# A cross-attention and feed-forward kernel: scores leave PSUM through a two-tensor product with a running maximum

## The chip, the cores and the metric

The kernel runs on one core of a Trainium2 chip. The metric is the device time of one execution in microseconds (us). Engines are named as in the profile: PE is the matrix engine, DVE the vector engine, ACT the scalar engine, POOL the GpSimd engine, and SP the engine that issues the DMAs.

## The reference

There are 1600 tokens of width 512, a context of 5776 rows of width 512, and 16 heads of width 32. What is computed, cut to what matters:

```
q = layernorm(x) @ Wq + bq            # 1600 x 512, per head 32
k, v = split(ctx @ Wkv + bkv)         # 5776 x 512 each
q = round_to_127_steps(q / sqrt(32))  # one step (scale) for each token and head
k = round_to_127_steps(k)             # one step for each key and head
v = round_to_127_steps(v)             # one step for each channel
attn = softmax(q @ k.T)               # per head 1600 x 5776
attn = round_to_255_steps(attn)       # scale: max(attn) / 255 of each row
x = x + (attn @ v) @ Wp + bp
x = x + ffn(layernorm(x))             # 512 -> 2 x 1408 -> 512, quantised, with an RMS norm
```

Because the rounded softmax row has its largest entry at 255, the kernel computes exp(s - max(s) + ln 255) and lets the write to an 8-bit integer do the rounding. The row sum of the exponentials divides the result later.

## The kernel before

**Stages.** First (to about 290 us) q is made for all tokens and k and v for the first group of four heads. Then comes the attention loop (about 290 to 1,780 us), and after it the output projection and the feed-forward part.

**The attention loop.** It has NA = 200 steps. A step `i` is one tile of 128 queries of one head (`tile_of`); for two heads at a time there are 25 steps, the last of which holds the two remainders of 64 queries. In a step the 5776 keys are taken in NC_ = 4 chunks of 1536, 1536, 1536 and 1168. For each chunk:

1. PE (`scores`, line 593) multiplies the queries `QT` with the keys `KT` into one of two PSUM buffers `PS`, up to three matmuls of 512 columns. It may write a buffer when the chunk two before has been evicted (semaphore `s_ev`).
2. DVE (line 967) evicts the chunk: it reads `PS`, multiplies by the query's step with its sign turned (`SQN`, or `SQP` in the tile of remainders), writes the negated scores as f32 to `S` in SBUF, and keeps their minimum in `MN`. The instruction is followed by a read of the accumulator.

After the four chunks DVE (line 982) forms `MS` = min of (`MN` + ln 255), which is the offset ln 255 - max(score), and signals `s_mx`. ACT (line 791) then computes exp(-S + MS) over the whole tile of 5888 columns to 8-bit integers `Pr`. The columns behind key 5776 hold `PAD_SCORE`, so that their exponential is 0. SP (line 464) transposes `Pr` by DMA to `PP`, POOL (line 1155) unpacks it to `PT` in four casts, and PE (`values`, line 612) multiplies it with the values `VI`, four steps (LAG) behind the scores. ACT (line 777) takes the product out of PSUM to `AO`, and PE waits for that (`s_pve`) before it writes `PO` again.

`S`, `MN`, `MS`, `Pr`, `PP` and `PT` have two buffers each. DVE may write `S[i % 2]` when the exponential of step i - 2 is done (`s_exp`).

**Beside it** the loop makes k and v of the next group of four heads, in 12 batches for each of three groups: PE lines 540 to 547, ACT lines 712 and 714 (out of PSUM), DVE lines 878 to 885 between two evictions, POOL lines 1091 to 1112, ACT lines 720 to 737. At a group's end POOL also quantises v (lines 1124 and 1127).

**Order.** Every engine has one queue, written out by hand in the order of the loops; an instruction that waits holds up all behind it on its engine. In ACT's queue a step is: the exponential, what is due of k (lines 737, 720 and 725), k and v out of PSUM for the next step, and the output of the tile i - 3 (line 777). In PE's queue each chunk's `scores` stand ahead of a quarter of `values(i - 4)`, and a part of the work for k and v stands behind.

Of the kernel before, what the change touches and what calls it, by code (L numbers as in the profile page):

```python
# [39 lines left out]
P = 128  # L40
# [24 lines left out]
PAD_SCORE = 1.0e30  # L65
# [48 lines left out]
class Chain:  # L114
# [13 lines left out]
    def link(self, ins):  # L128
        self.mark(ins)
        self.sync()  # L130


def build(nc, x, ctxt, ctxl, Wq, bq, Wkv, bkv, Wp, bp, w13T, w2T, norm_w, eye, Qd, Kd, Vd, Od, out):
    ctx = ExitStack()
    with ctx:
# [20 lines left out]
        MJ = sb("MJ", [P, NC_], F32)  # L156
        st = sb("st", [P, 2, 8], F32)
# [55 lines left out]
        with ExitStack() as unsplit:  # L213
# [27 lines left out]
                   s_kr s_kn s_ki s_kc s_k6 s_k8 s_kh s_kd s_kl s_kp s_vd0 s_vd1 s_vr s_vt s_vg s_vi s_wp s_qk s_ev s_mx s_exp s_pad s_pvp s_pv s_pve s_rz  # L241
# [456 lines left out]
        def _(act):  # L698
# [87 lines left out]
            for i in range(NA + LAG - 1):  # L786
                if i < NA:
                    act.wait_ge(M["s_mx"], i + 1)
                    if i >= 2:
                        act.wait_ge(s_tr[i % 2], 16 * (i // 2))  # L790
                    act.activation(Pr[i % 2].rearrange("p t q b -> p t b q"),  # L791
                                   S[i % 2].rearrange("p (t b q) -> p t b q", b=2, q=P), ACT.Exp, bias=MS[:, i % 2, 0:1],
                                   scale=-1.0, accum_out=ZB[:, i:i + 1]).then_inc(M["s_exp"], 1)
                for g, b in dve_batches.get(i - K_SPLIT, []):
                    k_high(g, b)
                for g, b in dve_batches.get(i - K_CAST, []):
                    k_round(g, b)
                for u in UNITS.get(i + 1, []):
                    unit_out(*u)
                if i >= LAG - 1:  # L800
                    values_out(i - LAG + 1)
# [49 lines left out]
        def _(v):  # L851
# [12 lines left out]
            link(v.memset(VF[:, (NU - 1) * P:KP], 0.0))  # L864
            v.memset(KS, 0.0).then_inc(M["cst"], 1)
# [51 lines left out]
            for t in range(NT):  # L917
# [13 lines left out]
                v.tensor_scalar(SQN[:, t, :], am[:, 1, :], -1.0 / 127.0, None, ALU.mult)  # L931
# [25 lines left out]
            for i in range(NA):  # L957
                p, segs = tile_of(i)
                h, q0 = segs[0][0], segs[0][1]
                neg_step = SQN[:, q0 // P, h:h + 1] if len(segs) == 1 else SQP[:, p:p + 1]  # L960
                if i >= 2:
                    v.wait_ge(M["s_exp"], i - 1)
                for c in range(NC_):
# [3 lines left out]
                    v.tensor_scalar(S[i % 2][:, c * CHUNK:c * CHUNK + CW[c]], PS[n % 2][:, 0:CW[c]], neg_step, None,  # L967
                                    ALU.mult, ALU.min, accum_out=MN[:, i % 2, c:c + 1]).then_inc(M["s_ev"], 1)
# [13 lines left out]
                v.tensor_scalar(MJ[:, :], MN[:, i % 2, :], LN255, None, ALU.add, ALU.min,  # L982
# [274 lines left out]
```

## Time and profile before

| what | before |
|---|---|
| median time (2 runs) | 2090.84 us (2090.33 to 2091.34) |
| profiled execution, its own time | 2093.51 us |
| its span | 2091.7 us |
| busy: PE, DVE, ACT, POOL | 1750.2, 1674.7, 1355.6, 1497.3 us |
| evictions, line 967 (with accumulator reads) | 1285.8 us |
| exponentials, line 791 | 1041.5 us |
| unpacking casts, line 1155 | 1096.2 us |
| score matmuls, line 593 | 789.5 us |
| TensorE's mean granted clock | 0.836 of full speed |

The profiled execution is 2.67 us longer than the median. Busy times are sums over records, and two DVE records can overlap by some tens of ns, so that DVE's real occupation is somewhat less than its busy share.

### The profile page before, as it was taken

The numbers are of one execution on the slowest core, as the hardware profiler recorded it, in microseconds if no ns is written. First come the engines' busy times: TensorE is split into PE (matmuls) and PEld (weight loads), VectorE is DVE, ScalarE is ACT, GpSimd is POOL, SyncE is SP. The second block draws the span as 40 slices with busy tenths as digits, with TensorE's granted clock in tenths as the row PEclk, the third lists the DMA queues.
The fourth block names the chain that finished last, engine by engine and source line by source line (L and its number), as shares of the span: only waits on it lengthen the run. The fifth ranks groups of instructions, "written<-read, shape, count | busy, mean of one in ns | idle before, by whom it ended". The sixth has DMA issues, their size and how long they took to land.

```text
span 2091.7 us, 40535 instructions
## 1 busy us (share of the span) xinstructions
PE 1750.2 (84%) x16230; PEld 1183.8 (57%) x16230; DVE 1674.7 (80%) x2664; ACT 1355.6 (65%) x1293; POOL 1497.3 (72%) x1182
## 2 busy tenths in 40 slices
PE   7765678898887888888788888978989889589997
PEld 6654456666565666655566665434444444367774
DVE  5433679999997999998799999989999999355552
ACT  2212268888868888887688888777777777332221
POOL 1211339888989888888898889988897987344543
PEclk9887789999898999988899999555555655699998
DMA  5333469999998989999988999897976875613221
GB/s 169 101 121 102 142 145 195 201 181 201 190 221 172 198 178 190 174 181 214 194 172 178 212 180 178 185 170 129 184 137 116 159 130 104 197 45 74 53 63 41
DMA packets 862442, 323.11 MB, mean 154 GB/s; under 512 B 789104, under 2 KB 817712, under 8 KB 862256
## 3 DMA queue, kind: packets, MB, share of 16 engines
q1 hardware_dynamic: 862256, 320.53, 73.5%
q8 instruction: 129, 2.11, 0.4%
q14 instruction: 57, 0.47, 0.1%
HBM read 80.87 MB, written 46.20 MB: 61 GB/s over the span
## 4 chain that ended last, share of the span: by engine, by line
DVE 34%; PE 26%; POOL 13%; issue 12%; DMA 7%; ACT 5%; SPq 3%; POOLq 0%; DVEq 0%; ACTq 0%
DVE S L967 30%; POOL PT L1155 8%; PE PS L593 6%; PE PS L654 5%; DMA PP<-Pr 3%; PE PK L540 3%; PE PK L688 3%; DMA k_rows<-KS 2%; PE PS L570 2%; PE PK L671 2%; ACT Pr L791 2%; PE PK L542 2%; PE PO L612 1%; POOL VQ L1124 1%; SPq L464 1%
## 5 line engine op out<-in xcount | busy, mean ns | idle before, releaser
L967 DVE TENSOR_SCALAR_CACHE_REDUCE S<-PS,SQN 128x1536 f32<-128x1536 f32 (+1 forms) x768 | 1285.8, 1714 | 93.4 <-PE PS L593 78.0
L791 ACT ACTIVATE Pr<-S,MS 128x5888 uint8<-128x5888 f32 x200 | 1041.5, 5207 | 245.0 <-DVE MJ L982 171.8
L1155 POOL CAST PT<-PP 128x1536 uint16<-128x1536 uint8 (+1 forms) x800 | 1096.2, 1416 | 94.5 <-DMA PP<-Pr 93.5
L593 PE MATMUL PS<-KT,QT 96*128 96x512 bf16 (+1 forms) x2496 | 789.5, 448 | 115.3 <-DVE S L967 101.7
L612 PEld LDWEIGHTS PO<-VI,PT 128*128 128x128 f16 x9200 | 365.3, 102 | 360.7 <-issue 188.4
L612 PE MATMUL PO<-VI,PT 128*128 128x32 bf16 x9200 | 376.7, 183 | 95.1 <-ACT AO L777 67.7
L593 PEld LDWEIGHTS PS<-KT,QT 96*128 96x128 bf16 (+1 forms) x2496 | 216.1, 108 | 314.6 <-issue 183.5
L540 PE MATMUL PK<-WG,CT 128*128 128x128 f32 (+1 forms) x1272 | 233.6, 316 | 85.3 <-ACT VF L714 56.4
L540 PEld LDWEIGHTS PK<-WG,CT 128*128 128x128 f32 (+1 forms) x1272 | 183.4, 210 | 90.8 <-issue 70.0
L542 PE MATMUL PK<-CT,WG 128*128 128x128 f32 (+1 forms) x1272 | 215.3, 298 | 0.0
L542 PEld LDWEIGHTS PK<-CT,WG 128*128 128x128 f32 x1272 | 171.5, 199 | 1.3 <-issue 0.5
L654 PE MATMUL PS<-W,XIF 128*128 128x512 f32 (+3 forms) x624 | 142.6, 384 | 4.1 <-POOL XIF L1210 4.1
L1112 POOL TENSOR_TENSOR KS<-KE 128x512 bf16<-128x512 f32 (+1 forms) x48 | 50.0, 1041 | 128.5 <-DMA k_rows<-KS 124.4
L654 PEld LDWEIGHTS PS<-W,XIF 128*128 128x128 f32 (+1 forms) x624 | 113.2, 186 | 31.2 <-POOL XIF L1210 6.1
L1091 POOL TENSOR_TENSOR KB<-KB,kam 128x512 f32<-128x512 f32 (+1 forms) x48 | 48.6, 1013 | 106.9 <-DVE kam L885 106.9
L737 ACT ACTIVATE KS<-KD 128x512 bf16<-128x512 bf16 (+1 forms) x48 | 29.2, 609 | 116.7 <-DMA k_rows<-KS 113.5
L712 ACT ACTIVATE KB<-PK 128x128 f32<-128x128 f32 (+1 forms) x159 | 42.7, 269 | 90.8 <-PE PK L542 89.9
L1103 POOL TENSOR_TENSOR KD<-KE,kam 128x512 f32<-128x512 f32 (+1 forms) x48 | 50.8, 1058 | 67.0 <-ACT KE L725 67.0
L906 DVE RECIPROCAL sd<-sd 128x1 f32<-128x1 f32 x13 | 2.1, 164 | 114.3 <-ACT sd L743 114.3
L688 PE MATMUL PK<-W,IQF 128*128 128x512 f32 (+1 forms) x286 | 71.9, 409 | 15.1 <-POOL IQF L1204 11.5
L688 PEld LDWEIGHTS PK<-W,IQF 128*128 128x128 f32 (+1 forms) x286 | 54.8, 193 | 29.5 <-POOL IQF L1204 12.4
L843 ACT ACTIVATE TG<-G 128x1408 f32<-128x1408 f32 (+1 forms) x13 | 17.9, 1377 | 79.9 <-DVE G L1044 79.9
(125 smaller groups left out, 1484.5 us busy)
## 6 DMA issues: line engine op xcount, KB each, us to landing
CT<-ctxt SPq DMA_DIRECT2D x180, 256.0 KB, 3.3
k_rows<-KS SPq DMA_DIRECT2D x44, 512.0 KB, 3.9
v_rows<-VS SPq DMA_DIRECT2D x33, 256.0 KB, 3.7
VQ<-v_rows SPq DMA_DIRECT2D x33, 256.0 KB, 3.7
q_rows<-QS SPq DMA_DIRECT2D x13, 512.0 KB, 3.0
W13F<-w13T SPq DMA_DIRECT2D x16, 352.0 KB, 4.2
attn_out<-AO SPq DMA_DIRECT2D x8, 416.0 KB, 4.5
PP<-Pr SPq DMA_TRANSPOSE x200, 5.9
```

The lines of the kernel that those rows point to most:

```text
L540: pe.matmul(bank[0:n, 0:GC], CT[k % RING][:, d, 0:n], WG[:, d, 0, :], start=(d == 0), stop=False)
L542: last = pe.matmul(bank[:, GC:GC + n], WG[:, d, 1, :], CT[k % RING][:, d, 0:n], start=(d == 0), stop=(d == NK - 1))
L593: last = pe.matmul(PS[n % 2][p0:p0 + r, f:f + w], QT[h % 3][0:PARTS * HD, q0:q0 + r], KT[h % 3][0:PARTS * HD, c * CHUNK + f:c * CHUNK + f ...
L612: last = pe.matmul(PO[:, 0:w], PT[i % 2][:, u, :].bitcast(F16), VI[g % 2][:, u, h * HD:h * HD + w], start=(u == 0), stop=(u == NU - 1))
L654: last = pe.matmul(PS[half][0:n, f:f + w], XIF[:, c, 0:n], W13[:, c, a, half * FF + f:half * FF + f + w], start=(c == 0 and a == 0), stop= ...
L688: last = pe.matmul(PK[0:n, :], IQF[:, k, 0:n], W2[:, k, a, :], start=(k == 0 and a == 0), stop=(k == NF - 1 and a == WPARTS - 1))
L791: act.activation(Pr[i % 2].rearrange("p t q b -> p t b q"), S[i % 2].rearrange("p (t b q) -> p t b q", b=2, q=P), ACT.Exp, bias=MS[:, i % ...
L967: v.tensor_scalar(S[i % 2][:, c * CHUNK:c * CHUNK + CW[c]], PS[n % 2][:, 0:CW[c]], neg_step, None, ALU.mult, ALU.min, accum_out=MN[:, i % ...
L1091: gp.tensor_tensor(KA, KA, kam[:, kb % 2, 1, 0:m].unsqueeze(2).to_broadcast([P, m, HD]), ALU.mult).then_inc(M["s_kn"], 1)
L1103: gp.tensor_tensor(v3(KD), v3(KE), kam[:, kb % 2, 0, 0:m].unsqueeze(2).to_broadcast([P, m, HD]), ALU.mult).then_inc(M["s_k6"], 1)
L1112: gp.tensor_tensor(KS[:, 0:n, :, 2 * HD:3 * HD].rearrange("p n h d -> p (n h) d"), v3(KE), top(KE), ALU.subtract).then_inc(M["s_kp"], 1)
L1155: gp.tensor_copy(PT[i % 2][:, 2 * t0:2 * t1, :].rearrange("p (t b) q -> p t b q", b=2), PP[i % 2][:, t0:t1, :].bitcast(U8).rearrange("p t ...
```

## The change

Five edits:

- The eviction of a chunk is another instruction, now at line 975: `S = (PS * ONE) * step`, with `ONE` a block of ones in SBUF as a second tensor, and a running maximum that starts at -1e30, written to `MN`. It has an accumulator read behind it.
- The sign of the step is positive, `S` holds the scores themselves, and `PAD_SCORE` is -1e30.
- The last reduction (line 991) is a maximum over the four entries of `MN`, multiplied by 1.0; ln 255 is no longer added in it.
- ACT makes the offset: a new instruction (line 792) computes `BS` = -`MS` + ln 255 on 128x1, signals `s_bs`, and the exponential waits for that, with scale 1 and offset `BS`. It stands behind the wait for `s_mx` and ahead of the wait for the transposition.
- At the start DVE fills `L255` (128x1) and `ONE` (128x1536) in the row of memsets that all engines wait for (`cst`).

```diff
-PAD_SCORE = 1.0e30
+PAD_SCORE = -1.0e30
@@ tensors
+        BS = sb("BS", [P, 2, 1], F32)
+        L255 = sb("L255", [P, 1], F32)
+        ONE = sb("ONE", [P, CHUNK], F32)
@@ scalar engine, attention loop
                     act.wait_ge(M["s_mx"], i + 1)
+                    act.activation(BS[:, i % 2, :], MS[:, i % 2, :], ACT.Identity, bias=L255[:, 0:1],
+                                   scale=-1.0).then_inc(M["s_bs"], 1)
                     if i >= 2:
                         act.wait_ge(s_tr[i % 2], 16 * (i // 2))
+                    act.wait_ge(M["s_bs"], i + 1)
                     act.activation(Pr[i % 2].rearrange("p t q b -> p t b q"),
-                                   S[i % 2].rearrange("p (t b q) -> p t b q", b=2, q=P), ACT.Exp, bias=MS[:, i % 2, 0:1],
-                                   scale=-1.0, accum_out=ZB[:, i:i + 1]).then_inc(M["s_exp"], 1)
+                                   S[i % 2].rearrange("p (t b q) -> p t b q", b=2, q=P), ACT.Exp, bias=BS[:, i % 2, 0:1],
+                                   scale=1.0, accum_out=ZB[:, i:i + 1]).then_inc(M["s_exp"], 1)
@@ vector engine, start
             link(v.memset(VF[:, (NU - 1) * P:KP], 0.0))
+            link(v.memset(L255[:, :], LN255))
+            link(v.memset(ONE[:, :], 1.0))
             v.memset(KS, 0.0).then_inc(M["cst"], 1)
@@ vector engine, quantisation of q
-                v.tensor_scalar(SQN[:, t, :], am[:, 1, :], -1.0 / 127.0, None, ALU.mult)
+                v.tensor_scalar(SQN[:, t, :], am[:, 1, :], 1.0 / 127.0, None, ALU.mult)
@@ vector engine, attention loop
-                neg_step = SQN[:, q0 // P, h:h + 1] if len(segs) == 1 else SQP[:, p:p + 1]
+                step_ = SQN[:, q0 // P, h:h + 1] if len(segs) == 1 else SQP[:, p:p + 1]
...
-                    v.tensor_scalar(S[i % 2][:, c * CHUNK:c * CHUNK + CW[c]], PS[n % 2][:, 0:CW[c]], neg_step, None,
-                                    ALU.mult, ALU.min, accum_out=MN[:, i % 2, c:c + 1]).then_inc(M["s_ev"], 1)
+                    v.tensor_tensor_reduce(S[i % 2][:, c * CHUNK:c * CHUNK + CW[c]], PS[n % 2][:, 0:CW[c]],
+                                           ONE[:, 0:CW[c]], step_, -1.0e30, ALU.mult, ALU.max,
+                                           accum_out=MN[:, i % 2, c:c + 1]).then_inc(M["s_ev"], 1)
...
-                v.tensor_scalar(MJ[:, :], MN[:, i % 2, :], LN255, None, ALU.add, ALU.min,
+                v.tensor_scalar(MJ[:, :], MN[:, i % 2, :], 1.0, None, ALU.mult, ALU.max,
                                 accum_out=MS[:, i % 2, 0:1]).then_inc(M["s_mx"], 1)
```

No instruction changes its place. On DVE the end of a step and the start of the next read so before (the accumulator reads, which the trace shows, are not listed here):

```order
L967 TENSOR_SCALAR S,MN<-PS,SQN 128x1536 x3
L967 TENSOR_SCALAR S,MN<-PS,SQN 128x1168
L982 TENSOR_SCALAR MJ,MS<-MN 128x4
L967 TENSOR_SCALAR S,MN<-PS,SQN 128x1536
L878 TENSOR_REDUCE kam<-KB 128x16
```

and so in the change, from a step's third chunk on:

```order
L975 ISA S,MN<-PS,ONE,SQN 128x1536
L975 ISA MN 128x1
L975 ISA S,MN<-PS,ONE,SQN 128x1168
L975 ISA MN 128x1
L991 TENSOR_SCALAR MJ,MS<-MN 128x4
L975 ISA S,MN<-PS,ONE,SQN 128x1536
L975 ISA MN 128x1
L886 TENSOR_REDUCE kam<-KB 128x16
```

The new eviction is a pair, the product and the read of the accumulator into `MN`. On ACT, at the start of the attention loop, the change reads:

```order
L792 ACTIVATE BS<-MS,L 128x1
L797 ACT_TABLE_LOAD
L797 ACTIVATE Pr,ZB<-S,BS 128x23x2x128
L715 ACTIVATE KB<-PK 128x4x32
L717 ACTIVATE VS<-PK,BV 128x128
L792 ACTIVATE BS<-MS,L 128x1
```

The small instruction `BS` is new in front of each exponential, and no further table load comes with it.

## Rows read from the trace of the kernel before

**Rows 1.** The page: the chain that ended last, by engine and by line.
```profile
DVE 34%; PE 26%; POOL 13%; issue 12%; DMA 7%; ACT 5%; SPq 3%; POOLq 0%; DVEq 0%; ACTq 0%
DVE S L967 30%; POOL PT L1155 8%; PE PS L593 6%; PE PS L654 5%; DMA PP<-Pr 3%; PE PK L540 3%; PE PK L688 3%; DMA k_rows<-KS 2%; PE PS L570 2%; PE PK L671 2%; ACT Pr L791 2%; PE PK L542 2%; PE PO L612 1%; POOL VQ L1124 1%; SPq L464 1%
```

**Rows 2.** Windows: stretch, length, busy time of each engine, granted clock, DMA share, GB/s.
```profile
590.00:660.00 70.00, 54.91 (x602) 38.50 (x601) 55.63 (x85) 47.29 (x44) 63.41 (x61) 0.88 1.01 200
...
1500.00:1779.00 279.00, 248.82 (x2344) 124.75 (x2342) 268.98 (x397) 212.34 (x122) 238.13 (x169) 0.55 0.71 132
sum 1489.00, PE 1291.55 PEld 828.84 DVE 1396.59 ACT 1202.54 POOL 1300.70; mean PE 143.51 PEld 92.09 DVE 155.18 ACT 133.62 POOL 144.52
```

**Rows 3.** Timeline of DVE in the loop: start, duration (us), line, operation.
```profile
303.54 1.82 DVE L967 TENSOR_SCALAR_CACHE_REDUCE S<-PS,SQN 128x1536 f32<-128x1536 f32 x1
305.28 0.08 DVE L967 DVE_READ_ACCUMULATOR S<-PS,SQN 128x1 f32 x1
...
310.33 1.82 DVE L967 TENSOR_SCALAR_CACHE_REDUCE S<-PS,SQN 128x1536 f32<-128x1536 f32 x1
...
312.08 0.70 DVE L878 TENSOR_REDUCE kam<-KB 128x16 f32<-128x528 f32 x1
312.69 1.81 DVE L967 TENSOR_SCALAR_CACHE_REDUCE S<-PS,SQN 128x1536 f32<-128x1536 f32 x1
```

**Rows 4.** DVE by line and form: count | busy us, mean ns of one | idle before.
```profile
L967 DVE TENSOR_SCALAR_CACHE_REDUCE S<-PS,SQN 128x1536 f32<-128x1536 f32 x576 | 1025.8, 1814 | 93.1 <-PE PS L593 77.9 <-ACT Pr L791 14.2 <-issue 0.6
L967 DVE TENSOR_SCALAR_CACHE_REDUCE S<-PS,SQN 128x1168 f32<-128x1168 f32 x192 | 271.6, 1414 | 0.3 <-PE PS L593 0.2
...
L1044 DVE SCALAR_TENSOR_TENSOR G<-PS,sc,TG 128x1408 f32<-128x1408 f32 x12 | 20.2, 1683 | 51.0 <-PE PS L654 51.0
...
L926 DVE TENSOR_TENSOR QF<-PS,BQ 128x512 f32<-128x512 f32 x13 | 9.0, 692 | 7.9 <-PE PS L570 7.5
...
L909 DVE TENSOR_SCALAR XN<-XT,mv,sd 128x512 f32<-128x512 f32 x13 | 7.1, 546 | 0.5
...
L1022 DVE TENSOR_SCALAR Y<-Y,sc 128x512 f32<-128x512 f32 x12 | 5.8, 487 | 0.4
```

**Rows 5.** Chain of waits, its pieces in order of time: start, us, what.
```profile
783.38 0.10 DVE MJ L982
...
783.52 5.08 issue
...
790.40 0.10 ACT AO L777
...
792.10 1.28 PE PS L593 x3
```

**Rows 6.** Timeline of DVE: the eviction that this chain reaches, idle before it.
```profile
793.42 1.82 DVE L967 TENSOR_SCALAR_CACHE_REDUCE S<-PS,SQN 128x1536 f32<-128x1536 f32 x1 [1.40 <-PE PS L593]
```

**Rows 7.** Chain of waits: the first and last exponential that follow line 982 on it.
```profile
399.98 5.08 issue
...
1771.39 5.30 ACT Pr L791 x2
```

**Rows 8.** ACT, line 743: durations in ns, least/median/most, first and last start.
```profile
L743 ACT ACTIVATE sd<-mv x13: 186/187/204, 17.3 to 220.7; 128x1 f32<-128x1 f32 x13
```

**Rows 9.** Waits over the span: us in total, times, longest us.
```profile
ACT Pr L791 <- DVE MJ L982: 171.8, 132, 2.1
```

**Rows 10.** Timelines of DVE and POOL while both work, 77 us.
```profile
77.30 0.69 DVE L926 TENSOR_TENSOR QF<-PS,BQ 128x512 f32<-128x512 f32 x1
...
77.35 1.05 POOL L1091 TENSOR_TENSOR KB<-KB,kam 128x512 f32<-128x512 f32 x1 [3.62 <-DVE kam L885]
```

**Rows 11.** DVE, line 933, both tensors in SBUF: least/median/most ns.
```profile
L933 DVE TENSOR_TENSOR QG<-QF,am x13: 691/1257/1257, 30.1 to 244.8; 128x512 f32<-128x512 f32 x13
```

**Rows 12.** Timeline at the start: the first work of DVE and PE behind the memsets.
```profile
9.66 2.08 PE L540 MATMUL PK<-WG,CT 128*128 128x128 f32 x8 [9.66 <-DVE KS L865]
...
14.79 0.69 DVE L902 BATCH_NORM_STATS2 st<-XT 128x6 f32<-128x512 f32 x1 [5.18 <-issue]
```

More of the change, by code:

```diff
@@ L240, in build @@
         names = """cst s_x0 s_x1 s_w s_sd s_xn s_tp s_tpe s_q s_qe s_qs s_qd0 s_qd1 s_wg s_wg1 s_bk0 s_bk1 s_bv s_ku s_kve
-                   s_kr s_kn s_ki s_kc s_k6 s_k8 s_kh s_kd s_kl s_kp s_vd0 s_vd1 s_vr s_vt s_vg s_vi s_wp s_qk s_ev s_mx s_exp s_pad s_pvp s_pv s_pve s_rz
+                   s_kr s_kn s_ki s_kc s_k6 s_k8 s_kh s_kd s_kl s_kp s_vd0 s_vd1 s_vr s_vt s_vg s_vi s_wp s_qk s_ev s_mx s_bs s_exp s_pad s_pvp s_pv s_pve s_rz
                    s_nrm s_un s_ao0 s_ao1 s_dve s_act s_pool
```

## The prediction

> **What bounds the kernel now.** I read the chain of waits first. By line, the DVE eviction (line 967) holds 30% of the 2091.7 us span, 628 us; POOL's cast (line 1155) has 8%, and the exponential only a few [rows 1]. The windows by stage then say where: the attention loop, 290 to 1,779 us, is 1,489 us long, and DVE's records fill 1,396.6 us of it, more than PE, ACT or POOL [rows 2]. The timeline of DVE gives the beat. An eviction of 1536 columns starts 1.74 us after the one before it (303.54 to 305.28), and a whole step takes 6.79 us (303.54 to 310.33) [rows 3]. Two hundred such steps are 1,358 us, and the small DVE reductions for k stand between them, as at 312.08.
>
> But the loop isn't DVE alone. At the end of a group of heads POOL is the bound: from 590 to 660 us it is busy 63.4 of 70 us, DVE 55.6 [rows 2]. Where a batch of k falls due, the chain runs from the last reduction (783.38) through the exponential (783.52, given as "issue" of 5.08 us) to ACT's output of PO (790.40) and PE's scores (792.10), which DVE has waited 1.40 us for [rows 5, 6]. Meanwhile DVE has evicted four chunks off the chain. And late in the loop, from 1,500 us on, the granted clock is 0.55 (near the lower level, 1.2 GHz) and PE is busy 249 of 279 us, DVE 269 [rows 2]: there PE is a close second. An eviction with its read is 1.64 us in the mean (1.74 for 1536 columns, and a step's 6.79 less three of these, for the last chunk and the final reduction together, is 1.57). So 628 us are about 380 of the 800 evictions. That is the weight: one ns more for each eviction costs 0.38 us of kernel, at least until the waits beside it are used up (the 1.40 us at 793 are 350 ns for each of four evictions).
>
> **The eviction itself.** No row has the new operation, a product of two tensors with a pointer scale and a running maximum. Its neighbours are these.
> - Today's, one tensor from PSUM with a pointer step and an accumulator: 1814 ns for 1536 columns and 1414 for 1168 [rows 4]. In between, by 400/368 = 1.087 ns a column, 1408 columns would take 1675 ns.
> - Line 1044: two tensors, one in PSUM and one in SBUF, and a pointer scalar, but no accumulator: 1683 ns for 1408 columns [rows 4].
>
> So the second stream costs 8 ns. That is the nearest row, it has the same operands, and I take it: 380 x 0.008 = 3.0 us. The read of the accumulator is there before (0.08 us, at 305.28 [rows 3]) and after, 800 times each. *Lower bound:* line 878, which has no accumulator, is followed by the next eviction after 0.61 us (312.08 to 312.69) for 528 columns [rows 3], less 0.57 at 1.087 ns a column; today's eviction has 1.74 less 1.67. So the columns leave little else in the beat than the read, and the new pair can save at most its 0.08 us: -30 us. *Upper bound without a change of rate:* its start value and scale take more setting up. A tensor_scalar with two pointers takes 546 ns, one with one 487 [rows 4], 59 ns for a pointer; two of them are 0.12 us: +45 us.
>
> The Trainium skill, in "Vector Engine (DVE) Microarchitecture Reference", section "Rate slope and fixed cost", states that the multi-step programs measured there paid the same fixed time for an instruction as built-in operations; by that the difference would be nil and the sum below 3.0 us less, and no row here shows it.
>
> **The accumulator with two sources.** What the rows exclude is a loss of rate from the second tensor alone: line 1044 runs at full rate. What they don't show is such an operation that also accumulates. The same page of the Trainium skill, under "Points that are easy to get wrong", warns that an operation of two 4-byte SBUF sources with the accumulator runs at half the rate, since both read ports are taken. Here one source is in PSUM, so the rule doesn't apply by its letter; it is the strongest word against this change and is priced below.
>
> **The offset on ACT.** 200 new instructions on 128x1. The nearest, line 743, takes 187 ns [rows 8]. The exponential waits for its semaphore, and 0.04 us pass between an event and the start that it frees (line 982 ends at 783.48, the exponential begins at 783.52 [rows 5]), so each exponential that starts at once on `MS` starts 0.23 us later. ACT waited for line 982 in 132 of the 200 steps [rows 9], but that costs only where the exponential is on the chain and follows line 982 directly: I count 20 such pieces, the first at 399.98, one at 783.52, the last at 1771.39 [rows 5, 7]. 20 x 0.23 = 4.6 us. Where the exponential waits for the transposition, `BS` is made ahead of that wait and costs nothing. Behind `BS` on ACT stand the exponential, the copies out of PSUM and `AO`; they move by 0.23 us, and PE and SP wait for them. Bounds: nothing if the exponentials' place on the chain is taken by others, 46 us if all 200 count.
>
> **Costed at nothing.** The last reduction has one operation exchanged for another on four columns. The sign of the step and the pad value are the same instructions with other constants. The two memsets delay PE's first matmul, which now comes at 9.66 behind twelve of them, 0.8 us each, and so two more are some 1.6 us; but DVE's first work waits for loads until 14.79, and 5.18 us before it are idle [rows 12]; that load covers them, and without that cover they would cost these 1.6 us. POOL: the cast works beside the evictions. Could the block of ones take its port? Line 926 also reads PSUM and SBUF, and at 77.30 it ran beside POOL's two-tensor line 1091 at 77.35 in 0.69 us, its mean of 692 ns [rows 4, 10]. Line 933, with both tensors in SBUF, goes from 691 to 1257 ns in most of its 13 runs [rows 11]. So the collision exists, and the PSUM form is outside it.
>
> **Sum.** 2093.5 (profiled execution) + 3.0 + 4.6 = 2101.1 us; the profiled execution is 2.7 above the median of the runs, so **2098 us** against 2090.84. A difference of 2% (42 us) is about what a measurement of this kernel can tell from no change.
>
> **Rivals.**
> 1. *More fixed time for each new eviction.* Mechanism: the setting up of the custom product isn't hidden behind its predecessor, on DVE at every chunk. Decides, for 2%, from (42 - 4.6) / 0.38 = 98 ns on. At 0.06 us it gives 2091 + 5 + 23 = 2119 us, at the upper bound of 0.12, 2141. For it: no row has this operation. Against: line 1044's 8 ns. Chance 0.17, of which 0.07 above 2133.
> 2. *Half rate*, or the collision of line 933 after all. 1.087 x 1536 = 1.67 us more for three chunks and 1.27 for the fourth, 6.28 us a step, 1256 us in all; less the 92 us in which DVE is idle in the loop: some 3,255 us. This is the skill's warning turned into a time. Against: line 1044 at full rate, line 926 undisturbed. Chance 0.07.
> 3. *ScalarE's new step decides.* Up to 200 x 0.23 = 46 us, 2137 us, if every exponential were on the chain. For: 132 waits on line 982. Against: ACT is busy 1202.5 of the loop's 1,489 us [rows 2], so that its queue has 1.4 us of slack a step. Likelier values are 2105 to 2125. Chance 0.05.
> 4. *A cheaper pair.* If the accumulator read no longer holds the next eviction, DVE gains up to 30 us and ACT gives back 5: 2066 us. Against: the change still has a read in each pair, and PE at the lower clock soon becomes the bound. Chance 0.11, of which 0.03 beyond 2% (2049), for which the granted clock would have to move too.
>
> **Numbers.** The forecast, an eviction within -5 to +35 ns of today's, has 0.60, its own range 2088 to 2111 us. With rival 1 (0.17), rival 3 (0.05), rival 4 (0.11) and rival 2 (0.07), the range 2075 to 2135 leaves out rival 2, the top of rival 1 (0.06) and the lower half of rival 4 (0.05), 0.18 in all. Slower by over 2%: rivals 1 (0.07), 2 (0.07), 3 (0.02), and 0.02 out of the forecast's own share, for a weight that grows; 0.18. Faster: 0.03. Within: 0.79.
>
> **What would show it.** The new eviction's start-to-start time at 1536 columns: 1.75 us confirms, 1.80 or more is rival 1, 3.4 is rival 2, 1.66 is rival 4. `BS` at about 0.19 us and exponentials that start 0.27 us (not 0.04) after the last reduction. The stall at a batch of k (1.40 us) longer by 0.2. The cast's mean on POOL unchanged; if it grows, the port is shared. The forecast is wrong if evictions that were off the chain come onto it, so that 0.38 is too small, or if PE's granted clock changes with the slower beat.

## The result, and the profile after

The changed kernel takes **2123.59 us** (median of 2 runs, 2122.43 to 2124.74) against 2090.84: a ratio of 1.0157, with a 95% interval of 1.0113 to 1.0200. Its profiled execution has a span of 2120.6 us, 28.9 more than before, and a mean granted clock of 0.824 where before had 0.836. The time lies in the predicted range, 2075 to 2135 us, and on the side of the forecast, but 25.6 us above it and outside the forecast's own range, 2088 to 2111. The sum had no term of that size.

The profile page of the changed kernel, its chain by engine and by line, answers to [rows 1]; then two of its groups:

```profile
DVE 32%; PE 28%; issue 13%; POOL 13%; DMA 6%; ACT 5%; SPq 2%; POOLq 0%; DVEq 0%; ACTq 0%
DVE S L975 28%; POOL PT L1164 9%; PE PS L596 6%; PE PS L657 5%; PE PK L543 4%; PE PK L691 3%; DMA PP<-Pr 2%; DMA k_rows<-KS 2%; PE PS L573 2%; PE PK L545 2%; PE PK L674 2%; PE PO L615 2%; ACT Pr L797 1%; POOL VQ L1133 1%; PE PO L543 1%
...
L1164 POOL CAST PT<-PP 128x1536 uint16<-128x1536 uint8 (+1 forms) x800 | 1094.5, 1413 | 108.3 <-DMA PP<-Pr 107.7
...
L792 ACT ACTIVATE BS<-MS,L 128x1 f32<-128x1 f32 x200 | 59.3, 296 | 160.6 <-DVE MJ L991 160.5
```

DVE's share of the chain fell and PE's rose. POOL's cast has 1413 ns in the mean, against 1416 before: unchanged. `BS` takes 296 ns.

The eviction, by form (it answers to [rows 4]):

```profile
L975 DVE CUSTOM_DVE_ANT_0 S<-PS,ONE,SQN 128x1536 f32<-128x1536 f32 x576 | 1026.6, 1813 | 116.8 <-PE PS L596 99.4 <-ACT Pr L797 15.7 <-issue 0.4
L975 DVE CUSTOM_DVE_ANT_0 S<-PS,ONE,SQN 128x1168 f32<-128x1168 f32 x192 | 271.3, 1413 | 0.2 <-PE PS L596 0.2
L975 DVE DVE_READ_ACCUMULATOR2_ANT MN<- 128x1 f32 x800 | 65.8, 82 | 0.0
```

And the timeline of DVE (it answers to [rows 3]):

```profile
320.62 1.82 DVE L975 CUSTOM_DVE_ANT_0 S<-PS,ONE,SQN 128x1536 f32<-128x1536 f32 x1
...
322.36 1.81 DVE L975 CUSTOM_DVE_ANT_0 S<-PS,ONE,SQN 128x1536 f32<-128x1536 f32 x1
```

The means are 1813 and 1413 ns against 1814 and 1414, and the beat is 1.74 us as before (320.62 to 322.36): the eviction costs the same. What grew is the first group's wait for PE's scores, 99.4 us against 77.9. So DVE isn't slower; it is fed later.

**Where in time.** Each step ends with DVE's last reduction `MJ` (line 982 before, 991 after). Its start, minus that of the same step before, gives the loss up to that step, in us (worked out from the timelines of the profiled executions; the last two columns say what each stretch adds):

| kernel | step 0 | 16 | 112 | 128 | 199 | steps 0 to 112 | 112 to 128 |
|---|---|---|---|---|---|---|---|
| changed | 1.8 | 2.5 | 14.0 | 21.4 | 28.5 | 12.2 | 7.5 |
| changed, second profile (changed_again) | 2.1 | 4.4 | 10.9 | 17.9 | 27.3 | 8.8 | 7.0 |

The stretch from step 112 to 128 (1152.6 to 1268.5 us before) is the plainest: 16 of 200 steps hold a quarter of the loss. The window 1150 to 1265, of before and then of the changed kernel (columns as in [rows 2]):

```profile
1150.00:1265.00 115.00, 101.31 (x1215) 72.20 (x1214) 112.94 (x172) 100.79 (x95) 102.97 (x81) 1.00 0.97 192
```

```profile
1150.00:1265.00 115.00, 101.29 (x1150) 71.94 (x1151) 105.96 (x159) 98.93 (x103) 98.13 (x77) 0.94 0.91 181
```

Before, the clock is at its higher level (2.4 GHz) throughout, and DVE is busy 98% of the time. Now the mean clock is 0.94. PE is as long busy with 5% fewer records, and DVE gets 7 us less work done. The timelines of PE show the place. First before, at a batch of k, which falls due about every fourth step, here in step 119 (start, duration, line, operation; in brackets the idle time before it and what ended it):

```profile
1193.97 0.81 PE L593 MATMUL PS<-KT,QT 96*128 96x512 bf16 x3 [0.38 <-DVE S L967]
1195.75 0.45 PE L612 MATMUL PO<-VI,PT 128*128 128x32 bf16 x12 [0.97 <-ACT AO L777]
1196.05 0.69 PE L540 MATMUL PK<-WG,CT 128*128 128x128 f32 x4
1196.58 0.81 PE L593 MATMUL PS<-KT,QT 96*128 96x512 bf16 x3
```

The same place in the changed kernel:

```profile
1209.87 0.81 PE L596 MATMUL PS<-KT,QT 96*128 96x512 bf16 x3 [0.38 <-DVE MN L975]
1212.02 0.45 PE L615 MATMUL PO<-VI,PT 128*128 128x32 bf16 x12 [1.34 <-ACT AO L780]
1212.32 1.19 PE L543 MATMUL PK<-WG,CT 128*128 128x128 f32 x4
1213.30 1.49 PE L596 MATMUL PS<-KT,QT 96*128 96x512 bf16 x3
```

PE waits for ACT's output of `PO`, which stands in ACT's queue behind the exponential and the k work. That wait is 0.37 us longer, and behind it the same matmuls take 1.19 and 1.49 us, not 0.69 and 0.81. The windows around this place in the changed kernel:

```profile
1208.00:1212.00 4.00, 2.30 (x22) 1.26 (x21) 3.97 (x7) 3.97 (x8) 0.56 (x1) 1.00 0.41 104
1212.00:1216.00 4.00, 3.98 (x37) 3.11 (x38) 2.23 (x3) 3.91 (x2) 3.84 (x4) 0.57 1.07 207
1216.00:1220.00 4.00, 3.90 (x50) 2.64 (x49) 3.72 (x5) 3.10 (x7) 4.00 (x4) 1.00 0.78 118
```

The granted clock goes from 1.00 to 0.57, near its lower level (1.2 GHz), and back. In those 4 us PE is busy without a break, and DVE, 2.23 of 4, waits for it. The timelines of DVE, before and then changed, show what that costs:

```profile
1197.43 1.82 DVE L967 TENSOR_SCALAR_CACHE_REDUCE S<-PS,SQN 128x1536 f32<-128x1536 f32 x1 [0.28 <-PE PS L593]
```

```profile
1214.83 1.82 DVE L975 CUSTOM_DVE_ANT_0 S<-PS,ONE,SQN 128x1536 f32<-128x1536 f32 x1 [1.77 <-PE PS L596]
...
1216.93 1.82 DVE L975 CUSTOM_DVE_ANT_0 S<-PS,ONE,SQN 128x1536 f32<-128x1536 f32 x1 [0.28 <-PE PS L596]
```

DVE waits 2.05 us in the two together, instead of 0.28: 1.8 us more at this batch, for 0.37 us of delay on ACT. Four batches fall into steps 112 to 128. At them DVE waits 7.9 us in all where it waited 1.1, so 6.7 of the 7.5 us are these waits. Before had such falls too, at other batches. This is PE in the kernel before, in front of the eviction of [rows 6]:

```profile
790.63 0.45 PE L612 MATMUL PO<-VI,PT 128*128 128x32 bf16 x12 [0.97 <-ACT AO L777]
790.93 1.17 PE L540 MATMUL PK<-WG,CT 128*128 128x128 f32 x4
791.89 1.49 PE L593 MATMUL PS<-KT,QT 96*128 96x512 bf16 x3
```

The prediction read the 1.40 us of that stall as a wait on ACT's chain that would grow by ACT's delay. Most of it was the lower clock: with the same 0.97 us of PE's idle time and the whole clock (1195.75) DVE waits only 0.28.

**The delay on ACT.** The timeline of ACT, where `BS` and the exponential both wait for nothing but line 991:

```profile
320.63 0.29 ACT L792 ACTIVATE BS<-MS,L 128x1 f32<-128x1 f32 x1 [1.48 <-DVE MJ L991]
321.02 5.21 ACT L797 ACTIVATE Pr<-S,BS 128x5888 uint8<-128x5888 f32 x1
```

The exponential starts 0.39 us after `BS` does. `BS` in turn starts 0.04 us after the last reduction's end (median), where the exponential itself started before.

### The profile page after: what moved, and what is told of

It reads as the page before. It is cut to its first block, busy times and chain, and to the rows that moved or that the text cites. A ratio compares the mean times of both kernels' runs of the same rounds, so it can differ in the third digit from the quotient of the medians.

```text
span 2120.6 us, 40737 instructions
## 1 busy us (share of the span) xinstructions
PE 1774.4 (84%) x16230; PEld 1195.4 (56%) x16230; DVE 1678.7 (79%) x2666; ACT 1411.1 (67%) x1493; POOL 1495.2 (71%) x1182
## 4 chain that ended last, share of the span: by engine, by line
DVE 32%; PE 28%; issue 13%; POOL 13%; DMA 6%; ACT 5%; SPq 2%; POOLq 0%; DVEq 0%; ACTq 0%
DVE S L975 28%; POOL PT L1164 9%; PE PS L596 6%; PE PS L657 5%; PE PK L543 4%; PE PK L691 3%; DMA PP<-Pr 2%; DMA k_rows<-KS 2%; PE PS L573 2%; PE PK L545 2%; PE PK L674 2%; PE PO L615 2%; ACT Pr L797 1%; POOL VQ L1133 1%; PE PO L543 1%
## 5 line engine op out<-in xcount | busy, mean ns | idle before, releaser
L975 DVE CUSTOM_DVE_ANT_0 S<-PS,ONE,SQN 128x1536 f32<-128x1536 f32 (+1 forms) x768 | 1286.6, 1713 | 117.1 <-PE PS L596 99.6
L1164 POOL CAST PT<-PP 128x1536 uint16<-128x1536 uint8 (+1 forms) x800 | 1094.5, 1413 | 108.3 <-DMA PP<-Pr 107.7
L797 ACT ACTIVATE Pr<-S,BS 128x5888 uint8<-128x5888 f32 x200 | 1041.3, 5206 | 63.2 <-DMA PP<-Pr 46.6
L596 PE MATMUL PS<-KT,QT 96*128 96x512 bf16 (+1 forms) x2496 | 804.7, 455 | 106.5 <-DVE MN L975 95.7
L596 PEld LDWEIGHTS PS<-KT,QT 96*128 96x128 bf16 (+1 forms) x2496 | 222.0, 109 | 303.9 <-issue 184.3
L543 PE MATMUL PK<-WG,CT 128*128 128x128 f32 (+1 forms) x1272 | 240.2, 323 | 85.7 <-ACT VF L717 53.3
L543 PEld LDWEIGHTS PK<-WG,CT 128*128 128x128 f32 (+1 forms) x1272 | 188.7, 216 | 90.9 <-issue 67.2
L792 ACT ACTIVATE BS<-MS,L 128x1 f32<-128x1 f32 x200 | 59.3, 296 | 160.6 <-DVE MJ L991 160.5
```

What stands on the lines that cost most here:

```text
L543: pe.matmul(bank[0:n, 0:GC], CT[k % RING][:, d, 0:n], WG[:, d, 0, :], start=(d == 0), stop=False)
L596: last = pe.matmul(PS[n % 2][p0:p0 + r, f:f + w], QT[h % 3][0:PARTS * HD, q0:q0 + r], KT[h % 3][0:PARTS * HD, c * CHUNK + f:c * CHUNK + f ...
L792: act.activation(BS[:, i % 2, :], MS[:, i % 2, :], ACT.Identity, bias=L255[:, 0:1], scale=-1.0).then_inc(M["s_bs"], 1)
L797: act.activation(Pr[i % 2].rearrange("p t q b -> p t b q"), S[i % 2].rearrange("p (t b q) -> p t b q", b=2, q=P), ACT.Exp, bias=BS[:, i % ...
L975: v.tensor_tensor_reduce(S[i % 2][:, c * CHUNK:c * CHUNK + CW[c]], PS[n % 2][:, 0:CW[c]], ONE[:, 0:CW[c]], step_, -1.0e30, ALU.mult, ALU.m ...
L1164: gp.tensor_copy(PT[i % 2][:, 2 * t0:2 * t1, :].rearrange("p (t b) q -> p t b q", b=2), PP[i % 2][:, t0:t1, :].bitcast(U8).rearrange("p t ...
```

## The experiments

The theories: **clock** (what costs is the step in PE's clock that ACT's small delay sets off at the batches of k), against **eviction** (the new DVE pair), **delay** (ACT's time adds up in proportion, rival 3 of the prediction) and **memsets**. In the recorded expectations "theory O" is ACT's offset with the clock behind it, and "theory E" is the eviction. Every ratio is against the kernel before on the same chip, where it had medians of 2094 to 2097 us. The column of steps is the one introduced above, from each run's profiled execution. Of one kernel it repeats well (7.5 and 7.0 us for the changed one).

| kernel | us | ratio (95%) | steps 112 to 128, us |
|---|---|---|---|
| changed_again | 2123.46 | 1.0127 (1.0109 to 1.0145) | +7.0 |
| bs_only | 2115.55 | 1.0103 (1.0082 to 1.0124) | +7.1 |
| evict_only | 2096.87 | 1.0010 (0.9993 to 1.0027) | +0.2 |
| bs_unread | 2109.31 | 1.0075 (1.0054 to 1.0095) | +6.7 |
| bs_copy | 2112.29 | 1.0093 (1.0071 to 1.0115) | +7.0 |
| bs_twice | 2132.05 | 1.0179 (1.0161 to 1.0196) | +9.2 |
| ones_late | 2121.69 | 1.0129 (1.0114 to 1.0144) | +7.6 |
| ao_first | 2087.43 | 0.9969 (0.9955 to 0.9983) | -1.3 |
| ao_first_after | 2109.15 | 1.0067 (1.0049 to 1.0086) | +5.0 |
| k_last | 2088.71 | 0.9966 (0.9951 to 0.9981) | -1.5 |
| k_last_after | 2096.45 | 1.0000 (0.9984 to 1.0016) | -1.2 |
| pe_fed | 2103.52 | 1.0039 (1.0025 to 1.0054) | +2.7 |

### Each half of the change alone

**evict_only** is the kernel before with the new kind of eviction, in a form that keeps the sign and the minimum:

```diff
-                    v.tensor_scalar(S[...], PS[...], neg_step, None, ALU.mult, ALU.min, accum_out=MN[...])
+                    v.tensor_tensor_reduce(S[...], PS[...], ZRO[:, 0:CW[c]], neg_step, 1.0e30,
+                                           ALU.add, ALU.min, accum_out=MN[...])
```

`ZRO` is a block of zeros, set at the start. Like the change's eviction it has a second tensor in SBUF, a start value and a pair of instructions. It differs from it by the addition of zeros in place of the product with ones, and by the minimum and the negative sign that are kept.

> The kernel before with the eviction alone exchanged: a two-tensor custom operation of the same family (sum with a block of zeros, times the negative step, running minimum), the offset still made by DVE. Theory O: 2091 to 2094 us (1.5 us of them the block's memset at the start), the pair's beat 1.74 us for 1536 columns. Theory E: 2115 to 2123 us.

Measured: 1.0010, no difference to be told. Its evictions, by form:

```profile
L969 DVE CUSTOM_DVE_ANT_0 S<-PS,ZRO,SQN 128x1536 f32<-128x1536 f32 x576 | 1025.9, 1814 | 92.2 <-PE PS L594 70.5 <-ACT Pr L792 19.6 <-issue 0.7
```

The **eviction** theory is out, as far as this form stands for the change's own: the pair and the memset of its block together cost at most 0.3% of the time.

**bs_only** is the other half, the offset on ACT with the old eviction:

```diff
+                    act.activation(BS[:, i % 2, :], MS[:, i % 2, :], ACT.Identity, bias=L255[:, 0:1],
+                                   scale=1.0).then_inc(M["s_bs"], 1)
...
+                    act.wait_ge(M["s_bs"], i + 1)
...
-                                   ... ACT.Exp, bias=MS[:, i % 2, 0:1], ...)
+                                   ... ACT.Exp, bias=BS[:, i % 2, 0:1], ...)
...
-                v.tensor_scalar(MJ[:, :], MN[:, i % 2, :], LN255, None, ALU.add, ALU.min,
+                v.tensor_scalar(MJ[:, :], MN[:, i % 2, :], 1.0, None, ALU.mult, ALU.min,
```

`L255` is filled at the start, as in the change; `S`, the pad and the exponential keep the old sign.

> The kernel before with the offset made by ScalarE alone: the eviction stays one tensor with a minimum, and only the 128x1 instruction and the wait for it are added. Theory O (the loss is the exponential's later start, 0.39 us after the small instruction's, which goes on through ACT's output of PO to PE and there lets the granted clock fall at the batches of k): nearly the whole loss, 2117 to 2123 us, and granted clock 1.0 alternating with dips between steps 112 and 136. Theory E (the two-tensor eviction costs something that its duration doesn't show, such as SBUF reads beside the other engines): 2091 to 2098 us.

Measured: 1.0103, some 20 us of the 27 that the whole change loses (changed_again, each against the kernel before on its own chip). Most of the loss sits on ACT.

### How the loss depends on ACT's delay

**bs_unread** makes `BS` and reads it nowhere: as bs_only, but the exponential keeps its old offset and has no new wait.

```diff
+                    act.activation(BS[:, i % 2, :], MS[:, i % 2, :], ACT.Identity, bias=L255[:, 0:1],
+                                   scale=1.0).then_inc(M["s_bs"], 1)
```

> The kernel before with the small instruction on ScalarE, whose result nobody reads and nobody waits for; it occupies ACT but the exponential need not wait for its end. If the loss is ACT's occupation (0.3 us busy in each step): 2115 us or more. If it is the round trip (end of the small instruction, semaphore, start of the exponential): the exponential starts some 0.1 to 0.2 us later instead of 0.39, and the time is 2093 to 2103 us.

**bs_copy** is the changed kernel with a cheaper form of `BS`, constants only:

```diff
-                    act.activation(BS[...], MS[...], ACT.Identity, bias=L255[:, 0:1], scale=-1.0)
+                    act.activation(BS[...], MS[...], ACT.Copy, bias=LN255, scale=-1.0)
```

> The changed kernel with the offset made by a Copy with constants in the instruction in place of a pointer offset: some 190 ns instead of 295, the exponential 0.28 us late instead of 0.39. Theory O in its plain form (a fixed share of the delay arrives): about 70% of the loss, 2113 us. Theory O with the granted clock as a step: either all of the 11 us between steps 112 and 136 stay (2115 to 2120 us) or they vanish together (2100 to 2108 us).

The timelines of ACT, of bs_unread and then of bs_copy:

```profile
319.33 0.29 ACT L791 ACTIVATE BS<-MS,L 128x1 f32<-128x1 f32 x1 [1.66 <-DVE MJ L987]
319.53 5.19 ACT L795 ACTIVATE Pr<-S,MS 128x5888 uint8<-128x5888 f32 x1
```

```profile
311.77 0.20 ACT L792 ACTIVATE BS<-MS 128x1 f32<-128x1 f32 x1
312.06 5.21 ACT L797 ACTIVATE Pr<-S,BS 128x5888 uint8<-128x5888 f32 x1
```

The exponential starts 0.2 us after `BS` does where nobody reads it, 0.3 with the cheap form, 0.4 in the change and in bs_only. If the delay itself were paid, the stretch of steps 112 to 128 would lose in the ratio 1 to 1.5 to 2. It loses 6.7, 7.0 and 7.1 to 7.5 us: in these steps nearly all of it comes with the first 0.2 us. That speaks for **clock** and against **delay**. PE in bs_unread, at a batch:

```profile
1200.67 0.45 PE L614 MATMUL PO<-VI,PT 128*128 128x32 bf16 x12 [1.16 <-ACT AO L779]
1200.97 1.19 PE L542 MATMUL PK<-WG,CT 128*128 128x128 f32 x4
1201.95 1.49 PE L595 MATMUL PS<-KT,QT 96*128 96x512 bf16 x3
```

0.19 us more of idle time than before are enough for the fall here, with the same 1.19 and 1.49 us behind it. Over the whole kernel the three stand in order (1.0075, 1.0093, 1.0103), but their intervals overlap. bs_copy differs from the changed kernel by 0.1 us of delay alone, and yet loses only 1.0093 against 1.0127. Where the difference comes from is shown below, in the comparison by batch.

**bs_twice** puts two such instructions in a row, each waiting for the one before:

```diff
-                    act.activation(BS[...], MS[...], ACT.Identity, bias=L255[:, 0:1], scale=-1.0).then_inc(M["s_bs"], 1)
+                    act.activation(BT[...], MS[...], ACT.Identity, bias=L255[:, 0:1], scale=-1.0).then_inc(M["s_bt"], 1)
+                    act.wait_ge(M["s_bt"], i + 1)
+                    act.activation(BS[...], BT[...], ACT.Identity).then_inc(M["s_bs"], 1)
```

> The changed kernel with a second small instruction in the chain, so that the exponential starts some 0.75 us late in place of 0.39. Theory O as a step that is already taken at 0.17 us, plus a share of each delay that arrives directly: 2130 to 2145 us (ratio 1.017 to 1.025). If the delay arrives in proportion in all stretches: twice the loss, 1.03.

Measured: 2132.05, 9 to 11 us above the changed kernel (by the medians, and by the ratios) for 0.23 us more of delay at each step (`BT` 305.03, exponential 305.65 in its trace, 0.62 against 0.39). The first 0.39 us had cost 20 (bs_only). So on the whole more delay does cost more, 4 to 5 us for each tenth of a us in both cases, and from the totals alone **delay** isn't refuted. The step shows in the stretch in which before has the full clock.

### Taking PE's wait away

**ao_first** is the kernel before with the output of `PO` directly behind the exponential in ACT's queue, and **ao_first_after** is the changed kernel with the same move:

```diff
+                if i >= LAG - 1:
+                    values_out(i - LAG + 1)
                 for g, b in dve_batches.get(i - K_SPLIT, []):
                     k_high(g, b)
...
-                if i >= LAG - 1:
-                    values_out(i - LAG + 1)
```

> The kernel before with ACT's output of PO (line 777) moved directly behind the exponential, ahead of the work for k and v. Theory O says that at a batch of k PE waits for this output behind 1.2 us of k work, idles, and falls to the lower clock, so that DVE waits 0.3 to 1.7 us a batch: with the output 1.2 to 1.9 us earlier, PE's waits for it at those steps go and the kernel gains 10 to 30 us (ratio 0.986 to 0.995). If ACT's queue as a whole is the path, not the place of the output in it: no change (0.998 to 1.002), since the same instructions stand in it.

> The changed kernel with the same move. Theory O: the 0.39 us of the offset are then covered by the 1.2 us won, and the time is within 8 us of ao_first (ratio to before 0.99 to 0.999). If the offset's delay reaches DVE by another way (occupation of ACT, the transposition of the exponentials), 15 us or more stay between the two.

Measured: 0.9969 and 1.0067. The first is a gain of some 7 us. The second still loses 15 us where the change loses 27: only part of the loss went. Its timeline of PE tells why:

```profile
1200.93 0.46 PE L615 MATMUL PO<-VI,PT 128*128 128x32 bf16 x12
1202.43 0.68 PE L543 MATMUL PK<-WG,CT 128*128 128x128 f32 x4 [1.04 <-ACT VS L717]
1202.95 1.33 PE L596 MATMUL PS<-KT,QT 96*128 96x512 bf16 x3
```

PE no longer waits for `AO`, but for the copies of k and v out of `PK` that now stand behind it, 1.04 us, and the clock falls all the same. At this place ao_first itself waits less, and keeps the clock:

```profile
1189.59 0.68 PE L540 MATMUL PK<-WG,CT 128*128 128x128 f32 x4 [0.67 <-ACT VS L714]
1190.11 0.81 PE L593 MATMUL PS<-KT,QT 96*128 96x512 bf16 x3
```

So it isn't that one wait: what PE needs stands behind ACT's k work in more than one place. Hence **k_last**: the k work itself (k_high, k_round) goes behind both, where the buffer `KB` allows it, in the kernel before, and **k_last_after** in the changed one. Both have this edit:

```diff
-                for g, b in dve_batches.get(i - K_SPLIT, []):
-                    k_high(g, b)
...
+                split, cast = dve_batches.get(i - K_SPLIT, []), dve_batches.get(i - K_CAST, [])
+                due = [g * NBT + u // NB for g, u in UNITS.get(i + 1, [])]
+                first = bool(due and cast) and max(due) > cast[0][0] * NBT + cast[0][1] + 1
...
```

Where `first` holds, k_high and k_round stay ahead; elsewhere unit_out and values_out go ahead of them.

> The kernel before with ACT's work for k (lines 737, 720 and 725) moved behind both kinds of copies out of PSUM, the output of PO and k and v, wherever the buffers of k allow it. PE then waits for neither at a batch of k. If the two waits are all that a batch costs DVE: the dips of the granted clock between 500 and 950 us go too, and the gain is larger than that of moving the output of PO alone (0.9969): 0.985 to 0.995. If the k work, now later by 0.6 us, delays the next exponential instead: 0.995 to 1.003.

> The changed kernel with the same move. With the output of PO alone moved, PE waited 1.04 us for k's copies instead and the clock still fell (1.0067 against before). Theory O: with both waits gone the granted clock is 1.0 from 1,130 to 1,290 us, DVE waits under 0.5 us a batch, and the ratio to before is 0.992 to 1.000. If it stays at 1.004 or above with the clock at 1.0, the offset's delay costs by another way, ACT's own time above all.

Measured: 0.9966 and 1.0000. The changed kernel, with nothing but the order of ACT's queue altered, is as fast as before. The windows of k_last_after, and its PE at a batch:

```profile
1150.00:1265.00 115.00, 102.65 (x1230) 72.76 (x1228) 114.00 (x174) 105.49 (x114) 103.09 (x80) 1.00 1.00 193
```

```profile
1185.12 0.81 PE L596 MATMUL PS<-KT,QT 96*128 96x512 bf16 x3 [0.38 <-DVE MN L984]
1186.09 0.45 PE L615 MATMUL PO<-VI,PT 128*128 128x32 bf16 x12 [0.15 <-ACT AO L780]
```

PE waits 0.15 us where it waited 1.34, the clock is whole, and DVE is busy 114 of 115 us. Between k_last and k_last_after there are 7.7 us, where the same change cost 27 in the old order. That is the change's price in an order in which PE hardly waits at the batches. By itself this pair doesn't part the clock from the wait, since both go.

**pe_fed** tests the clock directly. In the changed kernel PE makes the three score matmuls of a step's first chunk twice, ahead of its signal, at the steps where it would wait behind ACT's k work. It is only more work, on the same path:

```diff
+            def fed(i):
+                return bool(dve_batches.get(i - 2 - K_CAST) or dve_batches.get(i - 2 - K_SPLIT))
...
-                for f in range(0, CW[c], 512):
+                passes = 2 if c == 0 and fed(i) else 1
+                for f in list(range(0, CW[c], 512)) * passes:
```

> The changed kernel with more work for PE: at the steps in which PE waits behind ACT's k work, the three matmuls of the first chunk are made twice before they are signalled, so that PE is busy for 0.65 us of the 1.34 it would be idle. Clock theory (after the long idle the granted clock falls to the lower level and the next chunk is late by 1.5 us): more work, less time; the clock stays at 1.0 between 1,130 and 1,290 us, the 10 us of steps 112 to 136 come back, and the ratio to before is 1.003 to 1.009. Delay theory (only the 0.39 us count): no gain, 1.013 or more.

Measured: 2103.52 us, **20 us less** than the changed kernel on the same chip (2123.46), with 222 more matmuls. Its window, its PE and its DVE at a batch:

```profile
1150.00:1265.00 115.00, 103.59 (x1206) 72.24 (x1206) 110.80 (x167) 102.21 (x113) 100.05 (x79) 1.00 0.99 189
```

```profile
1195.04 1.46 PE L600 MATMUL PS<-KT,QT 96*128 96x512 bf16 x6 [0.38 <-DVE MN L979]
1197.19 0.45 PE L619 MATMUL PO<-VI,PT 128*128 128x32 bf16 x12 [0.69 <-ACT AO L784]
1197.49 0.69 PE L543 MATMUL PK<-WG,CT 128*128 128x128 f32 x4
1198.02 0.81 PE L600 MATMUL PS<-KT,QT 96*128 96x512 bf16 x3
```

```profile
1196.64 1.82 DVE L979 CUSTOM_DVE_ANT_0 S<-PS,ONE,SQN 128x1536 f32<-128x1536 f32 x1 [0.20 <-PE PS L600]
...
1198.87 1.82 DVE L979 CUSTOM_DVE_ANT_0 S<-PS,ONE,SQN 128x1536 f32<-128x1536 f32 x1 [0.40 <-PE PS L600]
```

ACT's order and its delay are those of the changed kernel. PE still waits for `AO`, but half as long, since it works for the rest. The clock stays at 1.00, the matmuls behind keep 0.69 and 0.81, and DVE waits 0.20 and 0.40 us where it waited 1.77 and 0.28. **Delay** can't explain a gain from added work. **Clock** can.

### The other batches

The same comparison can be made over the rest of the loop. This is DVE's wait for PE's scores in single steps with a batch, in us (sums from the timelines of DVE):

| step | before | changed | changed_again | bs_unread | bs_copy | pe_fed | k_last_after |
|---|---|---|---|---|---|---|---|
| 35 | 0.29 | 1.70 | 1.72 | 1.88 | 0.55 | 0.60 | 0 |
| 63 | 0.28 | 2.04 | 1.79 | 0.47 | 0.54 | 0.60 | 0 |
| 67 | 1.70 | 2.00 | 1.80 | 1.76 | 1.71 | 0.60 | 0.47 |
| 71 | 1.69 | 1.80 | 1.80 | 1.83 | 1.70 | 0.60 | 0 |
| 75 | 0.29 | 0.64 | 0.64 | 0.47 | 0.55 | 0.59 | 0 |
| 79 | 0.47 | 2.02 | 2.01 | 0.66 | 0.76 | 0.79 | 0 |
| 111 | 0.29 | 2.05 | 1.80 | 0.47 | 0.54 | 0.60 | 0 |
| 131 | 0.28 | 3.04 | 3.04 | 1.89 | 1.71 | 0.60 | 0 |

The small values belong to batches with the whole clock, the large ones to batches at which it fell: at step 63 the first chunk's score matmuls take 0.81 us before and 1.49 us (769.42) in the changed kernel. Where the clock falls in both (67, 71), the change adds only 0.1 to 0.3 us. Where it falls newly, it adds 1.4 us or more: steps 35, 63, 79 and 111 add 6.5 of the 12.2 us that are lost up to step 112 (6.0 of 8.8 in changed_again), and step 131 adds 2.8 more. In bs_copy, with 0.1 us less delay, none of 35, 63, 79 and 111 fell, and it loses 2.5 us up to step 112 instead of 8.8 to 12.2. So here more delay costs more largely because the clock falls at more batches. (Each column is one profiled execution.) Not every step goes that way: at step 59 DVE waited 3.81 us before, and 2.05 and 0.64 in the changed kernel's two profiles. pe_fed keeps the clock even at 67 and 71, where before lost it.

But the length of PE's wait alone doesn't decide. This is the changed kernel in step 103:

```profile
1088.40 0.51 PE L615 MATMUL PO<-VI,PT 128*128 128x64 bf16 x12 [1.34 <-ACT AO L780]
1088.75 0.69 PE L543 MATMUL PK<-WG,CT 128*128 128x128 f32 x4
1089.28 0.81 PE L596 MATMUL PS<-KT,QT 96*128 96x512 bf16 x3
```

PE waited 1.34 us, as in step 119, and the clock stayed whole.

### The memsets, and the whole again

**ones_late** is the changed kernel with the two memsets put behind the start:

```diff
-            link(v.memset(L255[:, :], LN255))
-            link(v.memset(ONE[:, :], 1.0))
... just ahead of the attention loop
+            link(v.memset(L255[:, :], LN255))
+            link(v.memset(ONE[:, :], 1.0))
```

> The changed kernel with the two memsets moved from the row that all engines wait for to DVE's queue just ahead of the attention loop. If they cost what the two traces differ by at the first step (1.8 us): ratio 0.001 below the changed kernel's, 1.009 to 1.015 against before, and the first final reduction at 281 us in place of 282.9. The prediction's claim that a load covers them: no difference at all.

Measured: 2121.69 us, 1.0129. Its first step ends 0.6 us later than before's, where the changed kernel had 1.8 and 2.1; but evict_only, with a memset of that size at the start, ends it 0.5 us earlier. So the first step scatters between profiled executions by as much as the memsets could cost, and in the median ones_late can't be told from changed_again. They are no part of the loss that can be told.

**changed_again** is the changed kernel unaltered, beside k_last, k_last_after and pe_fed.

> The changed kernel unaltered, beside the kernel before on the same chip as the other three. Measured first at 1.0157 (1.0113 to 1.02). Its parts gave 1.0103 (offset alone) and 1.001 (eviction alone), and late memsets took 0.002 to 0.003 off it. If the parts add up: 1.011 to 1.015.

Measured: 2123.46 us, 1.0127, below the first 1.0157 but inside its interval. The parts, 1.0103 for the offset, 1.0010 for the eviction, agree with the whole within their intervals.

## Why the prediction was right, and where it was not

- **The number.** It fell inside the range, but by luck as far as the mechanism goes: the forecast's own range ended at 2111, and the room up to 2135 came from rival 1, a dearer eviction, which didn't occur. The forecast was 7 us of loss, and the measured one is 33.
- **The eviction, 3.0 us.** Right, and a shade too dear. Its neighbour line 1044 priced the second tensor at 8 ns; it measured -1 ns (1813 against 1814), with a beat of 1.74 us (1.75 was forecast). Alone it gives 1.0010. The 1.64 us for an eviction with its read don't follow from the figures beside them, which give 1.70; with 1.35 us from the last chunk's start to its read (301.96 to 303.31 in the timeline of before) they do. Rival 1 needed 98 ns and is out, rival 4 too: the read of the accumulator, 82 ns, still stands in each pair.
- **Half rate, rival 2.** It didn't come, and the casts kept their time (1413 ns against 1416). The Trainium skill's warning ("Vector Engine (DVE) Microarchitecture Reference", "Points that are easy to get wrong") is for two sources in SBUF; the trace agrees that one in PSUM is outside it, with 1813 ns against 1814.
- **The offset on ACT, 4.6 us.** This is the term that was mis-sized: some 20 us (bs_only). The mechanism was named, later exponentials and PE waiting behind them, but two of its factors were wrong. The delay was taken from line 743, 187 ns, which has no pointer for its offset, so 0.23 with the 0.04 us of a semaphore; it measured 0.39, and the exponentials start 0.43 us after the last reduction, not the forecast 0.27 (medians). The Trainium skill states the difference in "ScalarE: Activation LUTs", "What ACT_TABLE_LOAD costs": each 128x1 pointer operand adds about 93 ns to 186. This case's medians are 295 ns with a pointer and 203 with constants (bs_copy), which agrees. And the weight was taken as the number of pieces on the chain, 20, each paid once. On the changed kernel's chain `BS` stands 28 times; even 28 x 0.39 = 10.9 us are only half of what the offset costs. At a batch of k the delay isn't paid once: 0.37 us more of PE's wait become 1.8 of DVE's where the clock falls. The prediction's last sentence named a change of PE's granted clock as what would make it wrong, and gave it no price.
- **A stall longer by 0.2 us.** The stall that it named, 1.40 us at 793.42 (step 67), became 1.78 us (1.80 in changed_again), longer by 0.4, about ACT's whole delay: there the clock had fallen before already. (With the next chunk's wait it is 1.70 against 2.00 and 1.80.) The stalls of 0.28 us, which it didn't look at, became up to 2.05.
- **Rival 3** ended nearest, with its likelier 2105 to 2125 us. It named the right engine, for the wrong reason: ACT isn't the bound (k_last_after has the same work on it and takes 1.0000).
- **The memsets, at nothing.** The cover named was the load that DVE waits for, and DVE's first work was indeed no later (14.47 us, 14.79 before [rows 12]). But PE has no load to wait for, and its first matmul came 1.85 us later (1.6 was the estimate):

```profile
11.51 2.08 PE L543 MATMUL PK<-WG,CT 128*128 128x128 f32 x8 [11.51 <-DVE KS L873]
```

PE stands on the chain in front of the loop, so DVE's load didn't cover it. Whether the 1.85 us reached the end isn't settled (ones_late).
- **Last reduction, sign, pad.** Nothing of theirs showed; `MJ` has 157 ns before and after.

**What stays open.** Why the clock falls at one batch and not at the next, no run here tells. In before it fell at 790.63 and not at 1195.75, with 0.97 us of idle PE at both; in the changed kernel it stayed with 1.34 us in step 103. The batches named above make up 16 of the changed kernel's 28.5 us (15 of 27.3 in changed_again). Of the rest, 1.8 us stand at the first step (2.1), and some 3 us come at steps 184 to 192, where DVE waits 2.6 us once for an exponential. It does so in bs_only (2.9) and evict_only (2.2) alike, and not in before; why is open. The remaining 8 us or less are a net sum and were not taken apart. Profiled executions differ here by several us up to step 112: 12.2 and 8.8 for the same changed kernel, and evict_only, which takes as long as before, gains 3.0 there.

## What to carry to other kernels

A delay on an engine off the path is to be followed to PE's idle time and then to PE's clock, not only to the chain: ask at each wait of PE what the matmuls behind it would take at the lower level (here 1.19 and 1.49 us for 0.69 and 0.81), and who waits for them. Before removing or adding small instructions, look at what the queue's order makes PE wait for; here the order of ACT's queue decided whether the same change cost 1.3% or nothing. A small instruction is priced by a row with the same kinds of operands, above all its pointers, and with its reader's wait.

## What the runs showed of the hardware that was not expected

- At step 119, 0.37 us more of idle time on PE (0.97 to 1.34) went with the lower clock for the next matmuls, and cost DVE 1.8 us. With idle times of 0.15, 0.67, 0.69 and 0.97 there the clock stayed; with 1.04 (ao_first_after), 1.16 (bs_unread) and 1.34 it fell. It is no rule: at other batches it fell with 0.97 (790.63) and stayed with 1.34 (step 103).
- Three redundant matmuls of 512 columns (0.65 us, 1.46 less 0.81) at some steps, 222 in all, made the kernel 20 us faster.
- An ACT instruction on 128x1 that nobody reads still moves the next one by 0.2 us, less than its own 0.29.
- The custom product with one tensor in PSUM and one in SBUF and a running maximum ran as long as the built-in operation with one tensor, to a nanosecond (1813 and 1814 ns for 1536 columns).
